# A sandwich layer (rotary linear attention, then a mixture of experts) on one core: transposes in pairs between products, the end in another order of products, its second weights split on the spot, and the residual of the early groups added by GpSimd

## The chip, the cores and the metric

One core of a Trainium2 chip. The kernel is one program with its own five instruction streams (TensorE is PE, its weight load PEld; VectorE is DVE; ScalarE is ACT; GpSimd is POOL; SyncE is SP and only issues transfers). The time is the device time of one execution in microseconds; lower is better.

## The reference, cut to what matters

X has 2 batches of 2048 tokens with 512 features, all in float32. `ln` is a layer norm over the features.

```
h   = ln(ln(X)) * ln_w + ln_b
Q, K, V = split(h @ W_in + b_in)           # 512 -> 3 * 512
Q, K = rope(Q), rope(K)
A   = sum over tokens of K / |K| * V       # one vector for a batch
x2  = X + ln(A * Q @ W_out + b_out + ln(X))
n3  = ln(x2)
gates: the two largest of n3 @ gate_w (8 experts), softmax over the two
routed = sum of gate * (gelu(n3 @ w1[e] + b1[e]) @ w2[e] + b2[e])
shared = gelu(n3 @ shared_w1 + shared_b1) @ shared_w2 + shared_b2
out = x2 + ln(routed + shared)
```

## The kernel before, in words

The 4096 tokens are 32 tiles of 128, in 8 groups of 4 tiles. Each float32 product is made of three products of split operands: a tensor is written as `hi` (rounded to float32r by an ACT copy) and `lo` (the rest, by a subtraction on DVE or POOL), and `product` (L1505) runs hi by hi, hi by lo and lo by hi over the 4 blocks of the contraction, so 12 matmuls of 512 columns. A "turn" brings a group from tokens on partitions to features on partitions by 16 transposes of 128 by 128, four to a PSUM bank, over two banks (`tp`). So the third set of four waits until the first bank has been emptied, and the fourth for the second.

**Front (0 to 322 us), a loop over 8 groups.** PE does for group g: for each of 4 tiles the K product and the V product (`kv`), then the turn of group g + 1, then four Q products (`q`, two banks). ACT empties the turn: for each k a copy with scale and bias into `hb`, and a rounding into `h_hi` (`front_split`), and POOL subtracts (`front_lo`, L1372), with two `hb` buffers, so the third ACT copy waits for POOL's first subtraction. ACT then takes the Q products out (`bias_q`) and rounds, in groups 1 to 5, four units of expert weights per group (`unit_hi`, L659: with tile 0, with tile 2, and behind Q products 0 and 2). DVE adds bias and rotates K, multiplies K by V, subtracts weight units (`unit_lo`, L943), and rotates Q together with POOL (`rc` on DVE at L925, `rsn` on POOL at L1391, which waits for Q products 0 and 1). Each engine takes its list in the order in which it is written. POOL adds K times V into `acc` (L1384).

**Attention (322 to 600 us), a loop over 8 steps.** Step s: four `attend` (a product with W_out and a bias row, into 3 banks), behind the third of them `n3_turn(s - 1)`, the transposes of the normed group before (`n3`, written by ACT at L714), then the gate's logits, and in most steps a quarter of the shared expert's work for the five EARLY groups (0, 2, 4, 6, 7): their first or their second product. ACT rounds the turn (`n_hi`), DVE subtracts (`n_lo_parts`, behind the third `z_tile`). Then the routing is worked out.

**Experts (627 to 893 us).** 71 tiles of 128 rows are gathered by indirect DMA, taken through their expert, and added into `f_scratch` by indirect DMA.

**The end (893 to 991 us).** The shared expert for the three LATE groups (1, 3, 5), as h0, o0, h1, o1, h2, o2 (`places`): `late_h(i)` is four products with the first shared weights, `late_turn(i + 1)` follows each h, `late_o(i)` is four products with the second weights (`c2_hi`, `c2_lo`, loaded ready split from scratch, 2 MB). Each h or o has four places m. Beside them DVE takes statistics of the EARLY tiles (`early_tile`, table `measured`; f is loaded by SP, one transfer of 1 MB for each group) and adds and measures the LATE ones (`late_tile`), POOL takes the roots (L1479), DVE the shifts, ACT norms the tile (`normed`, L827, table `normed_in`), and POOL issues a transfer that adds the tile to `out` in memory, where x2 lies already (`add_to_out`, L1486, 28 tiles). For the last group alone x2 is loaded (`x2c`), DVE adds it, and SP stores (L583). h and o of a group share one pair `hc_hi`, `hc_lo`, so ACT's first rounding of h(i) waits for the last product of o(i - 1).

Of the kernel before, what the change touches and what calls it, by code (L numbers as in the profile page):

```python
# [22 lines left out]
def sandwich_kernel(nc, X, ln_w, ln_b, W_in, b_in, W_out, b_out, gate_w, w1, b1, w2, b2,  # L23
# [51 lines left out]
    with ctx:  # L75
# [143 lines left out]
        hc_hi, hc_lo = at("hc_hi", 148, [P, KS, G], F32R), at("hc_lo", 156, [P, KS, G], F32R)  # L219
        x2c = at("x2c", 164, [P, GT, D])  # L220
# [51 lines left out]
        places = [(what, i, m) for i in range(len(LATE)) for what in ("h", "o") for m in range(GT)]  # L272
# [6 lines left out]
        measured = beside((0, 0, 2, 2, 1, 1, 1, 1, 2, 2, 2, 2, 1, 1, 1, 1) + (0,) * 8)  # L279
        normed_in = beside((0, 0, 0, 0, 0, 0, 2, 2, 0, 0, 1, 1, 2, 2, 2, 2, 1, 1, 1, 1, 1, 1, 0, 0))  # L280
# [20 lines left out]
        HALF_SET, ONES_SET, PICK_SET, GATE_ZERO, F_ZERO, ZEROS_SET = range(1, 7)  # L301
# [21 lines left out]
        bo_set, bo_hi_done, bo_split = sem("bo_set"), sem("bo_hi_done"), sem("bo_split")  # L323
        o_full, o_free, o_seen = sem("o_full"), sem("o_free"), sem("o_seen")
# [25 lines left out]
        c_in = [sem(f"c_in{i}") for i in range(3)]  # L350
# [5 lines left out]
        y_normed, y_added, stored, late_stored = sem("y_normed"), sem("y_added"), sem("stored"), sem("late_stored")  # L356
# [4 lines left out]
        def _(sp):  # L361
# [204 lines left out]
            sp.dma_start(c1_hi[:, :, :].rearrange("p k h -> p (k h)").bitcast(F32), ws_dram[0, 0]).then_inc(c_in[0], 16)  # L566

            for i in range(NRT - 1):
                sp.wait_ge(r_stored[i % NRO], 16 * (i // NRO + 1))
                sp.sem_inc(r_landed, 1)  # L570
            load_f(EARLY[0])
            load_f(EARLY[1])
            load_f(LATE[0])
            load_f(EARLY[2])
            load_f(EARLY[3])
            load_n3(2)
            load_f(LATE[1])
            load_f(EARLY[4])
            load_f(LATE[2])
            sp.dma_start(x2c[:, :, :], out_groups[LATE[2]]).then_inc(f_in[LATE[2]], 16)  # L580
            for j in range(GT):
                sp.wait_ge(y_added, j + 1)
                sp.dma_start(out_tiles[GT * LATE[2] + j], f[LATE[2]][:, j, :]).then_inc(late_stored, 16)  # L583
            sp.wait_ge(late_stored, 16 * GT)
            sp.wait_ge(stored, 16 * (NT - GT))

        @block.scalar
        def _(act):
# [9 lines left out]
            def front_split(f, u):  # L598
                for k in range(KD):
# [20 lines left out]
            def bias_q(g):  # L620
                for m in range(KD):
# [6 lines left out]
                    if m % 2 == 0:  # L628
                        unit_hi_in(g, 2 + m // 2)
# [41 lines left out]
            act.wait_ge(bo_set, 1)  # L671
# [141 lines left out]
            def gelu_c(i, m):  # L813
                n = KS * i + m
                act.wait_ge(sc_full, n + 1)
                if n >= 2:
                    act.wait_ge(hc_split, n - 1)
                act.activation(hsc[m % 2][:, :], sc[m if i == 0 else m % 2][:, :], ACT.Gelu, bias=sb1c[:, m:m + 1]).then_inc(sc_free, 1)
                if m == 0 and i > 0:
                    act.wait_ge(fc_full, GT * i)  # L820
                act.wait_ge(sc_free, n + 1)
                act.activation(hc_hi[:, m, :], hsc[m % 2][:, :], ACT.Copy).then_inc(hc_hi_done, 1)
# [7 lines left out]
            def load_c(n, i, c, w):  # L830
                act.dma_start(w[:, :, :].rearrange("p k h -> p (k h)").bitcast(F32), ws_dram[i, c]).then_inc(c_in[n], 16)
# [3 lines left out]
            load_c(1, 0, 1, c1_lo)  # L835
            scale_row(PRE)
            act.dma_start(n3c[1][:, :, :], n3_groups[LATE[1]]).then_inc(n3c_in[1], 16)
            load_c(2, 1, 0, c2_hi)
            load_c(2, 1, 1, c2_lo)
            for what, i, m in places:  # L840
                if what == "h":
                    gelu_c(i, m)
                if what == "h" and m == KS - 1 and i + 1 < len(LATE):
# [7 lines left out]
        def _(dve):  # L851
# [115 lines left out]
            for g in range(NG):  # L967
                k_tile(g, 0)
                v_tile(g, 0)
                if g == 0:  # L970
                    for n in range(2 * KD, 3 * KD):
                        lo_part(n)
                    dve.memset(bo[:, :].bitcast(F32), 0.0).then_inc(bo_set, 1)
                    dve.wait_ge(bo_hi_done, 1)
                    dve.wait_ge(bo_set, 1)
                    dve.tensor_tensor(bo[B_LO:B_LO + 1, :], bo_raw[B_LO:B_LO + 1, :], bo_hi[B_LO:B_LO + 1, :].bitcast(F32),
                                      ALU.subtract).then_inc(bo_split, 1)
# [78 lines left out]
            def n_lo_parts(g):  # L1056
                for k in range(KD):
# [38 lines left out]
            for s in range(NG):  # L1096
# [3 lines left out]
                z_tile(s, 1)  # L1100
                z_tile(s, 2)
                if s >= 1:
                    n_lo_parts(s - 1)
# [192 lines left out]
            def hc_lo_part(i, m):  # L1296
                dve.wait_ge(hc_hi_done, KS * i + m + 1)
                dve.tensor_tensor(hc_lo[:, m, :], hsc[m % 2][:, :], hc_hi[:, m, :].bitcast(F32), ALU.subtract)\
                   .then_inc(hc_split, 1)
# [16 lines left out]
            def early_tile(g, j):  # L1316
                if j == 0:
                    dve.wait_ge(f_in[g], 16)
# [15 lines left out]
            def add_x2(j):  # L1334
                g = LATE[-1]
                dve.wait_ge(y_normed, y_use[g, j] + 1)
                dve.tensor_tensor(f[g][:, j, :], f[g][:, j, :], x2c[:, j, :], ALU.add).then_inc(y_added, 1)

            waiting = []
            for what, i, m in places:  # L1340
                if what == "h":
                    hc_lo_part(i, m)
                else:
# [16 lines left out]
        def _(pool):  # L1360
# [120 lines left out]
            def add_to_out(g, j):  # L1481
                if g == LATE[-1]:
                    return
                pool.wait_ge(y_normed, y_use[g, j] + 1)
                pool.sem_inc(may_gather, 1)
# [13 lines left out]
        def _(pe):  # L1499
# [12 lines left out]
            def turn(f):  # L1512
                pe.wait_ge(h_normed, f + 1)
                for k in range(KD):
# [69 lines left out]
            def n3_turn(g):  # L1584
# [3 lines left out]
                for k in range(KD):  # L1588
# [47 lines left out]
            for s in range(NG):  # L1636
                attend(s, 0)
                attend(s, 1)
                attend(s, 2)
                if s >= 1:  # L1640
                    n3_turn(s - 1)
# [95 lines left out]
            for i in range(1, PRE + 1):  # L1737
# [5 lines left out]
                else:  # L1743
                    pe.wait_ge(n3c_in[0], 16)
# [29 lines left out]
            def late_h(i):  # L1774
                pe.wait_ge(tc_free, 4 + KD * (i + 1))
                if i == 0:
# [4 lines left out]
                    pe.wait_ge(c_in[1], 16)  # L1781
# [8 lines left out]
            def late_o(i):  # L1790
                pe.wait_ge(hc_split, KS * (i + 1))
                for j in range(GT):
# [3 lines left out]
                    product(oe_ps[n % 2][:, :], lambda k: hc_hi[:, k, c], lambda k: hc_lo[:, k, c],  # L1796
# [3 lines left out]
            pe.wait_ge(c_in[0], 16)  # L1800
            for i in range(len(LATE)):
                late_h(i)
                if i + 1 < len(LATE):
                    late_turn(i + 1)
                if i == 0:
                    pe.wait_ge(c_in[2], 32)
                late_o(i)
# [60 lines left out]
```

## Time and profile before

| | |
|---|---|
| median of 3 runs | 993.66 us (993.62 to 996.82) |
| the profiled execution's own time | 993.31 us |
| its span, first to last instruction | 991.5 us |
| PE busy | 894.3 us, 90% of the span |
| DVE, ACT, POOL busy | 632.4, 434.6, 399.7 us |
| mean granted TensorE clock | 0.974 of full speed |

The time holds about 2 us that lie outside the span. An idle gap of PE is read from PEld, the weight load that goes ahead of each matmul: the ends of matmuls are modelled and overlap the next start. In brackets behind a row stands how long its engine sat idle before it, and what ended that.

### The profile page before, as it was taken

Reading aid. Unit: us, or ns where it says so; the run is one execution under the profiler, and the core shown is the slowest. Engines: PE = TensorE matmul, PEld = TensorE weight load, DVE = VectorE, ACT = ScalarE, POOL = GpSimd, SP = SyncE. Lnnn points to the kernel's source line nnn. Section 1 sums busy time; section 2 is a strip of 40 time slices with the busy share of each in tenths; the row PEclk is TensorE's granted clock in tenths of the full one; section 3 lists DMA queues with packets and bytes.
Section 4 is the critical chain, followed back from the end, with each engine's and each line's share of the span. In section 5 each row is a group of like instructions: output and inputs, shape, how many; then the busy total and the mean of one; then the engine's idle time right before and its main releaser. Section 6 shows DMA issues by size and latency. Waiting matters only on the chain.

```text
span 991.5 us, 14758 instructions
## 1 busy us (share of the span) xinstructions
PE 894.3 (90%) x4558; PEld 733.2 (74%) x4558; DVE 632.4 (64%) x1358; ACT 434.6 (44%) x825; POOL 399.7 (40%) x328
## 2 busy tenths in 40 slices
PE   1998988988999899899999798699999999996985
PEld 1877877877878577677777686688888888884874
DVE  5757967966956755556566658466666566662774
ACT  4135345344342243131231435466666666663453
POOL 3356456455454000000000000376767676751463
PEclk9999999999999899999999999699999999999998
DMA  8226878778544795955533589387888777869988
GB/s 288 86 86 235 289 261 297 271 272 305 191 170 170 296 340 195 356 213 219 205 127 128 203 327 321 116 214 150 149 144 160 145 146 138 158 97 331 344 133 157
DMA packets 86842, 209.03 MB, mean 211 GB/s; under 512 B 11480, under 2 KB 19928, under 8 KB 81392
## 3 DMA queue, kind: packets, MB, share of 16 engines
q1 hardware_dynamic: 61760, 159.21, 44.4%
q0 software_dynamic: 19936, 44.65, 25.0%
q10 hardware_dynamic: 5072, 4.23, 1.5%
q8 instruction: 41, 0.67, 0.3%
q14 instruction: 33, 0.27, 0.1%
HBM read 117.05 MB, written 91.01 MB: 210 GB/s over the span
## 4 chain that ended last, share of the span: by engine, by line
PE 52%; DVE 9%; ACT 5%; DMA 5%; issue 3%; POOL 1%; DVEq 0%; ACTq 0%; SPq 0%; POOLq 0%
PE bank L1507 7%; PE bank L1508 7%; PE bank L1509 7%; PE bank L1703 4%; PE bank L1701 3%; PE bank L1702 3%; PE bank L1688 3%; PE bank L1718 3%; PE bank L1720 3%; PE bank L1719 3%; PE bank L1710 2%; DMA c_lo<-shared_scratch 2%; PE bank L1502 1%; DMA f_scratch<-fo 1%; PE bank L1621 1%
## 5 line engine op out<-in xcount | busy, mean ns | idle before, releaser
L1456 POOL DMA_INDIRECT f_scratch<-ro,dst x71 | 112.5, 1584 | 51.2 <-SPq L570 23.6
L1507 PE MATMUL bank<-wkv_hi,h_hi 128*128 128x512 f32 x256 | 100.6, 393 | 3.8 <-issue 3.8
L1448 POOL DMA_INDIRECT xr<-n_scratch,ids x71 | 70.0, 986 | 76.7 <-issue 48.4
L1508 PE MATMUL bank<-wkv_lo,h_hi 128*128 128x512 f32 x256 | 100.3, 392 | 0.0
L1509 PE MATMUL bank<-wkv_hi,h_lo 128*128 128x512 f32 x256 | 100.2, 391 | 0.0
L1260 DVE TENSOR_TENSOR ro<-bank,b2b 128x512 f32<-128x512 f32 x71 | 49.1, 692 | 65.7 <-PE bank L1720 54.3
L1701 PE MATMUL bank<-we,x_hi 128*128 x284 | 86.4, 304 | 0.3 <-DVE x_lo L1240 0.3
L1703 PE MATMUL bank<-we,x_lo 128*128 x284 | 80.5, 284 | 0.0
L1702 PE MATMUL bank<-we,x_hi 128*128 x284 | 80.5, 283 | 0.0
L613 ACT ACTIVATE sq<-kb 128x512 f32<-128x512 f32 x32 | 20.2, 633 | 117.1 <-DVE kb L905 117.1
L1377 POOL TENSOR_TENSOR rn<-ssq,half 128x1 f32<-128x1 f32 x32 | 27.5, 860 | 86.2 <-ACT sq L613 86.2
L1425 POOL TENSOR_TENSOR zr<-zv,half 128x4 f32<-128x4 f32 x8 | 8.1, 1009 | 134.1 <-DVE zv L1030 134.1
L1507 PE MATMUL bank<-wo_hi,q_hi 128*128 128x512 f32 x128 | 54.4, 425 | 7.4 <-DMA q_lo<-q_scratch 3.7
L1507 PEld LDWEIGHTS bank<-wkv_hi,h_hi 128*128 128x128 f32 x256 | 48.5, 190 | 14.3 <-issue 4.2
L1718 PE MATMUL bank<-we,g_hi 128*128 x142 | 56.5, 398 | 1.4 <-DVE g_lo L1252 1.3
L714 ACT ACTIVATE n<-z,xnm,xr__76 128x512 f32<-128x512 f32 x32 | 23.5, 804 | 77.2 <-DVE xnm L1053 77.2
L1507 PE MATMUL bank<-h_hi,wq_hi 128*128 128x512 f32 x128 | 51.3, 401 | 5.9 <-ACT qb L626 5.9
L1720 PE MATMUL bank<-we,g_lo 128*128 x142 | 56.4, 397 | 0.0
L1509 PEld LDWEIGHTS bank<-wkv_hi,h_lo 128*128 128x128 f32 x256 | 48.5, 189 | 10.2
L1719 PE MATMUL bank<-we,g_hi 128*128 x142 | 56.0, 394 | 0.0
L1508 PEld LDWEIGHTS bank<-wkv_lo,h_hi 128*128 128x128 f32 x256 | 48.5, 189 | 10.0
L1384 POOL TENSOR_TENSOR acc<-acc,prod 128x512 f32<-128x512 f32 x32 | 50.1, 1565 | 13.2 <-DVE prod L918 13.2
(226 smaller groups left out, 2523.0 us busy)
## 6 DMA issues: line engine op xcount, KB each, us to landing
xg<-in_X SPq DMA_DIRECT2D x16, 1024.0 KB, 7.8
we<-expert_scratch SPq DMA_DIRECT2D x6, 2048.0 KB, 12.6
w_lo<-in_w SPq DMA_DIRECT2D x16, 512.0 KB, 5.3
expert_scratch<-w_hi SPq DMA_DIRECT2D x16, 512.0 KB, 2.6
expert_scratch<-w_lo SPq DMA_DIRECT2D x16, 512.0 KB, 4.1
q_scratch<-qh SPq DMA_DIRECT2D x8, 1024.0 KB, 3.9
q_scratch<-qb SPq DMA_DIRECT2D x8, 1024.0 KB, 6.0
q_hi<-q_scratch SPq DMA_DIRECT2D x8, 1024.0 KB, 4.8
```

The costliest lines, as they stand in the source:

```text
L1384: pool.tensor_tensor(a, a, prod[j % 2][:, :], ALU.add).then_inc(acc_done, 1)
L1448: pool.indirect_dma_start(xr[u][:, :], None, n3_dram, bass.IndirectOffsetOnAxis(ids[:, i:i + 1], 0)).then_inc(row_in[u], 16)
L1456: pool.indirect_dma_start(f_dram, bass.IndirectOffsetOnAxis(dst[:, i:i + 1], 0), ro[i % NRO][:, :], None, compute_op=ALU.add).then_inc(r_s ...
L1507: pe.matmul(dst, hi(k), w_hi(k), start=(k == 0), stop=False)
L1508: pe.matmul(dst, hi(k), w_lo(k), start=False, stop=False)
L1509: last = pe.matmul(dst, lo(k), w_hi(k), start=False, stop=(k == KD - 1 and not more))
L1701: pe.matmul(out_h, x_hi[u][:, s], part_of(e, 0, k, H), start=(k == 0), stop=False)
L1702: pe.matmul(out_h, x_hi[u][:, s], part_of(e, 1, k, H), start=False, stop=False)
L1703: last = pe.matmul(out_h, x_lo[u][:, s], part_of(e, 0, k, H), start=False, stop=(k == KD - 1))
L1718: pe.matmul(oe_ps[u][:, :], g_hi[u][:, s], part_of(e, 2, k, D), start=(k == 0), stop=False)
L1719: pe.matmul(oe_ps[u][:, :], g_hi[u][:, s], part_of(e, 3, k, D), start=False, stop=False)
L1720: last = pe.matmul(oe_ps[u][:, :], g_lo[u][:, s], part_of(e, 2, k, D), start=False, stop=(k == KH - 1))
```

## The change: what it does

**Pairs of transposes.** In the front the first two sets of the turn of group g + 1 stand ahead of the last V product of group g and the other two behind Q product 0; in attention two sets stand ahead of the third `attend` and two ahead of the fourth. ACT takes the front's sets 0 and 1, Q product 0, sets 2 and 3, then Q products 1 to 3, with the weight units behind products 1 and 2; DVE takes `n_lo` in pairs ahead of and behind the third `z_tile`.

**The end.** The order is h0, h1, o0, h2, o1, o2, with two buffers of `hc_hi` and `hc_lo`; statistics and norms of EARLY tiles stand later in it (7 are measured by the end of o0, 11 in h2, 2 in o1; 10 of the 20 are normed in o1 and 4 in o2). `shared_w2` is loaded raw (1 MB) and split by ACT and DVE beside h1. For all five EARLY groups x2 is loaded by SP (5 MB more; statistics of a group now wait for f and x2), POOL adds it with 20 `tensor_tensor`, and SP stores those tiles; only the 8 tiles of groups 1 and 3 still go out by POOL's adding transfer. n3 of group 5 is loaded from ACT's queue, right behind the raw weights.

```diff
-        places = [(what, i, m) for i in range(len(LATE)) for what in ("h", "o") for m in range(GT)]
+        late_order = (("h", 0), ("h", 1), ("o", 0), ("h", 2), ("o", 1), ("o", 2))
+        places = [(what, i, m) for what, i in late_order for m in range(GT)]
-        measured = beside((0, 0, 2, 2, 1, 1, 1, 1, 2, 2, 2, 2, 1, 1, 1, 1) + (0,) * 8)
-        normed_in = beside((0, 0, 0, 0, 0, 0, 2, 2, 0, 0, 1, 1, 2, 2, 2, 2, 1, 1, 1, 1, 1, 1, 0, 0))
+        measured = beside((0,) * 6 + (2, 2, 0, 1, 1, 1, 2, 3, 3, 3, 1, 1) + (0,) * 6)
+        normed_in = beside((0,) * 8 + (0, 1, 1, 1, 1, 0, 1, 1, 2, 2, 3, 3, 2, 2, 0, 0))
...
             load_f(EARLY[0])
+            load_x2(EARLY[0])
+            load_f(LATE[0])
             load_f(EARLY[1])
-            load_f(LATE[0])
+            load_x2(EARLY[1])
...
+            sp.wait_ge(tc_full, 2 * KD)
+            load_x2(EARLY[3])
+            load_f(EARLY[4])
+            sp.wait_ge(tc_full, 3 * KD)
+            load_x2(EARLY[4])
             load_f(LATE[1])
-            load_f(EARLY[4])
+            sp.wait_ge(c_split, KS)
             load_f(LATE[2])
...
+            mine = [(g, j) for g, j in y_order if g not in LATE[:2]]
+            for g, j in mine[:6]:
+                store_y(g, j)
+            sp.wait_ge(sc_full, KS * len(LATE))
+            load_x2(LATE[2])
+            for g, j in mine[6:]:
+                store_y(g, j)
...
-                    front_split(g + 1, (g + 1) % 2)
-                    bias_q(g)
+                    front_split(g + 1, (g + 1) % 2, (0, 1))
+                    bias_q(g, (0,))
+                    front_split(g + 1, (g + 1) % 2, (2, 3))
+                    bias_q(g, (1, 2, 3))
...
                 pool.wait_ge(y_normed, y_use[g, j] + 1)
+                if g in EARLY:
+                    pool.tensor_tensor(f[g][:, j, :], f[g][:, j, :], x2c[g][:, j, :], ALU.add).then_inc(e_added, 1)
+                    return
                 pool.sem_inc(may_gather, 1)
                 pool.dma_start(out_tiles[GT * g + j], f[g][:, j, :], accum_op=ALU.add).then_inc(stored, 16)
...
+                    if j == GT - 1 and g + 1 < NG:
+                        turn(g + 1, (0, 1))
                     kv(g, j, 1)
-                if g + 1 < NG:
-                    turn(g + 1)
...
                 for m in range(KD):
                     q(g, m)
+                    if m == 0 and g + 1 < NG:
+                        turn(g + 1, (2, 3))
...
                 attend(s, 1)
+                if s >= 1:
+                    n3_turn(s - 1, (0, 1))
                 attend(s, 2)
                 if s >= 1:
-                    n3_turn(s - 1)
+                    n3_turn(s - 1, (2, 3))
```

## Rows read from the trace of the kernel before

**Rows 1.** Busy time by stretch: PE, PEld, DVE, ACT, POOL; clock; DMA share, GB/s.
```profile
400.00:500.00 100.00, 92.67 (x411) 71.22 (x410) 56.98 (x157) 26.56 (x41) 6.04 (x6) 0.98 0.63 235
...
910.00:920.00 10.00, 4.36 (x11) 3.48 (x12) 6.02 (x14) 0.09 (x1) 0.07 (x1) 0.66 1.05 388
...
940.00:950.00 10.00, 7.86 (x36) 6.42 (x35) 8.34 (x21) 5.36 (x9) 4.17 (x4) 0.83 0.70 126
```
**Rows 2.** Waits of the weight load, whole span: total, times, longest.
```profile
PEld bank L1502 <- ACT hb L604: 18.1, 16, 4.5
...
PEld bank L1502 <- DVE n_lo L1060: 13.8, 15, 2.3
...
PEld bank L1507 <- ACT qb L626: 8.8, 7, 1.6
```
**Rows 3.** Timeline of the weight load, front: turns and Q products.
```profile
51.76 0.42 PEld L1502 LDWEIGHTS bank<-ident,hn 128*128 128x128 f32 x4 [0.91 <-ACT hb L604]
58.24 0.19 PEld L1507 LDWEIGHTS bank<-h_hi,wq_hi 128*128 128x128 f32 x1 [0.76 <-ACT qb L626]
...
198.53 1.03 PEld L1502 LDWEIGHTS bank<-ident,hn 128*128 128x128 f32 x8
...
237.21 1.02 PEld L1502 LDWEIGHTS bank<-ident,hn 128*128 128x128 f32 x8
...
274.93 1.03 PEld L1502 LDWEIGHTS bank<-ident,hn 128*128 128x128 f32 x8
```
**Rows 4.** Timelines of POOL and DVE, groups 2 and 3 of the front.
```profile
131.82 2.61 POOL L1372 TENSOR_TENSOR h_lo<-hb,h_hi 128x512 fp32r<-128x512 f32 x2 [0.37 <-ACT h_hi L609]
...
134.63 1.23 DVE L943 TENSOR_TENSOR w_lo<-w_lo,w_hi 128x1024 fp32r<-128x1024 f32 x1 [7.04 <-ACT w_hi L659]
...
135.30 2.81 POOL L1391 TENSOR_TENSOR rsn<-qb,rf 128x1024 f32<-128x1024 f32 x1 [0.87 <-issue]
...
135.77 3.43 DVE L925 TENSOR_TENSOR rc<-qb,rf 128x1024 f32<-128x1024 f32 x1
...
147.71 0.69 DVE L896 TENSOR_TENSOR kb<-bank,bkv 128x512 f32<-128x512 f32 x1 [0.38 <-PE bank L1509]
```
**Rows 5.** Timeline of the weight load, attention, step 3.
```profile
415.87 0.18 PEld L1582 LDWEIGHTS bank<-bo,ones_f 64*128 64x128 f32 x1 [0.35 <-issue]
...
419.23 0.18 PEld L1582 LDWEIGHTS bank<-bo,ones_f 64*128 64x128 f32 x1 [0.35 <-issue]
...
421.88 0.42 PEld L1502 LDWEIGHTS bank<-ident,n 128*128 128x128 f32 x4 [1.37 <-DVE n_lo L1060]
```
**Rows 6.** Timeline of ACT, the same step.
```profile
414.16 2.94 ACT L714 ACTIVATE n<-z,xnm,xr__76 128x512 f32<-128x512 f32 x4 [21.05 <-DVE xnm L1053]
```
**Rows 7.** The end: timelines of ACT, DVE and the weight load.
```profile
908.05 2.04 ACT L790 ACTIVATE nc_hi<-bank 128x512 fp32r<-128x512 f32 x4
...
913.66 1.29 DVE L1319 BATCH_NORM_STATS2 fst<-f 128x6 f32<-128x512 f32 x2 [6.02 <-DMA f<-f_scratch]
914.86 0.68 DVE L1298 TENSOR_TENSOR hc_lo<-hsc,hc_hi 128x512 fp32r<-128x512 f32 x1
...
915.61 0.29 PEld L1507 LDWEIGHTS bank<-c_hi,hc_hi 128*128 128x128 f32 x1 [7.93 <-issue]
...
923.36 0.68 DVE L1329 TENSOR_TENSOR f<-bank,f 128x512 f32<-128x512 f32 x1
...
926.07 0.69 DVE L1329 TENSOR_TENSOR f<-bank,f 128x512 f32<-128x512 f32 x1
...
983.56 0.69 DVE L1329 TENSOR_TENSOR f<-bank,f 128x512 f32<-128x512 f32 x1
```
**Rows 8.** POOL's adds of 128 by 512 in the front: ns, least, median, most.
```profile
L1384 POOL TENSOR_TENSOR acc<-acc,prod x32: 1262/1292/2210, 42.7 to 314.2; 128x512 f32<-128x512 f32 x32
```
**Rows 9.** Timeline of POOL in the end.
```profile
933.18 5.34 POOL L1486 DMA_DIRECT2D out<-f  x6
...
985.47 0.57 POOL L1479 TENSOR_TENSOR fr<-fv,half 128x1 f32<-128x1 f32 x1 [1.31 <-DVE fv L1307]
```

More of the change, by code:

```diff
@@ L218, in sandwich_kernel @@
         hsc = [at(f"hsc{i}", 144 + 2 * i, [P, G]) for i in range(2)]
-        hc_hi, hc_lo = at("hc_hi", 148, [P, KS, G], F32R), at("hc_lo", 156, [P, KS, G], F32R)
-        x2c = at("x2c", 164, [P, GT, D])
+        hc_hi, hc_lo = ([at(f"{n}{i}", kb_ + 24 * i, [P, KS, G], F32R) for i in range(2)] for n, kb_ in (("hc_hi", 148), ("hc_lo", 156)))
+        x2c = {g: at(f"x2c{g}", kb_, [P, GT, D]) for g, kb_ in zip(EARLY + LATE[-1:], (164, 96, 128, 64, 72, 136))}
+        c2_raw = at("c2_raw", 8 * LATE[-1], [P, KS, D])
         fst, fmv = at("fst", 192.125, [P, NT, 6]), at("fmv", 193, [P, NT, 2])
@@ L348, in sandwich_kernel @@
         gate_ready, r_gated, r_landed = sem("gate_ready"), sem("r_gated"), sem("r_landed")
-        c_in = [sem(f"c_in{i}") for i in range(3)]
+        c_in, c_hi_done, c_split = [sem(f"c_in{i}") for i in range(2)], sem("c_hi_done"), sem("c_split")
         n3c_in, f_in = [sem(f"n3c_in{i}") for i in range(len(LATE))], [sem(f"f_in{g}") for g in range(NG)]
@@ L570, in _, with load_x2, store_y @@
                 sp.sem_inc(r_landed, 1)
+            def load_x2(g):
+                sp.dma_start(x2c[g][:, :, :], out_groups[g]).then_inc(f_in[g], 16)
+            def store_y(g, j):
+                if g in EARLY:
+                    sp.wait_ge(e_added, e_tiles.index((g, j)) + 1)
+                else:
+                    sp.wait_ge(y_added, j + 1)
+                sp.dma_start(out_tiles[GT * g + j], f[g][:, j, :]).then_inc(y_stored, 16)
             load_f(EARLY[0])
+            load_x2(EARLY[0])
+            load_f(LATE[0])
             load_f(EARLY[1])
-            load_f(LATE[0])
+            load_x2(EARLY[1])
             load_f(EARLY[2])
+            load_x2(EARLY[2])
             load_f(EARLY[3])
-            load_n3(2)
+            sp.wait_ge(tc_full, 2 * KD)
[3 more added lines that the diff above has]
+            load_x2(EARLY[4])
             load_f(LATE[1])
-            load_f(EARLY[4])
+            sp.wait_ge(c_split, KS)
             load_f(LATE[2])
[L580 to L585, printed above, removed]
+            mine = [(g, j) for g, j in y_order if g not in LATE[:2]]
[5 more added lines that the diff above has]
+                store_y(g, j)
+            sp.wait_ge(y_stored, 16 * len(mine))
+            sp.wait_ge(stored, 16 * 2 * GT)
         @block.scalar
@@ L596, in hi_part, with front_split @@
                 act.activation(dst, stage[n][:, :], ACT.Copy).then_inc(w_hi_done, 1)
-            def front_split(f, u):
-                for k in range(KD):
+            def front_split(f, u, ks=range(KD)):
+                for k in ks:
                     n = KD * f + k
@@ L618, in unit_hi_in, with bias_q @@
                     unit_hi(UG * (g - 1) + i)
-            def bias_q(g):
-                for m in range(KD):
+            def bias_q(g, ms=range(KD)):
+                for m in ms:
                     n = q_use(g, m)
@@ L818, in gelu_c @@
                 act.activation(hsc[m % 2][:, :], sc[m if i == 0 else m % 2][:, :], ACT.Gelu, bias=sb1c[:, m:m + 1]).then_inc(sc_free, 1)
-                if m == 0 and i > 0:
-                    act.wait_ge(fc_full, GT * i)
+                if m == 0 and i > 1:
+                    act.wait_ge(fc_full, GT * (i - 1))
                 act.wait_ge(sc_free, n + 1)
-                act.activation(hc_hi[:, m, :], hsc[m % 2][:, :], ACT.Copy).then_inc(hc_hi_done, 1)
+                act.activation(hc_hi[i % 2][:, m, :], hsc[m % 2][:, :], ACT.Copy).then_inc(hc_hi_done, 1)
             def normed(g, j):
@@ L842, in _ @@
                     gelu_c(i, m)
+                if (what, i) == ("h", 1):
+                    c2_hi_part(m)
                 if what == "h" and m == KS - 1 and i + 1 < len(LATE):
@@ L1054, in x2_shift, with n_lo_parts @@
                    .then_inc(xnm_ready, 1)
-            def n_lo_parts(g):
-                for k in range(KD):
+            def n_lo_parts(g, ks=range(KD)):
+                for k in ks:
                     n = t2_use(g, k)
@@ L1336, in add_x2, with c2_lo_part @@
                 dve.wait_ge(y_normed, y_use[g, j] + 1)
-                dve.tensor_tensor(f[g][:, j, :], f[g][:, j, :], x2c[:, j, :], ALU.add).then_inc(y_added, 1)
+                dve.tensor_tensor(f[g][:, j, :], f[g][:, j, :], x2c[g][:, j, :], ALU.add).then_inc(y_added, 1)
+            def c2_lo_part(k):
+                dve.wait_ge(c_hi_done, k + 1)
+                dve.tensor_tensor(c2_lo[:, k, :], c2_raw[:, k, :], c2_hi[:, k, :].bitcast(F32), ALU.subtract)\
+                   .then_inc(c_split, 1)
             waiting = []
@@ L1510, in product, with turn @@
                 return last
-            def turn(f):
+            def turn(f, ks=range(KD)):
                 pe.wait_ge(h_normed, f + 1)
-                for k in range(KD):
+                for k in ks:
                     n = KD * f + k
@@ L1587, in n3_turn @@
                     pe.wait_ge(tp_free, 2 + KD * NG)
-                for k in range(KD):
+                for k in ks:
                     n = t2_use(g, k)
@@ L1795, in late_o @@
                     c = slice(j * P, (j + 1) * P)
-                    product(oe_ps[n % 2][:, :], lambda k: hc_hi[:, k, c], lambda k: hc_lo[:, k, c],
+                    product(oe_ps[n % 2][:, :], lambda k: hc_hi[i % 2][:, k, c], lambda k: hc_lo[i % 2][:, k, c],
                             lambda k: c2_hi[:, k, :], lambda k: c2_lo[:, k, :]).then_inc(fc_full, 1)
             pe.wait_ge(hc_free, NRT - 1)
[L1800 to L1807, printed above, removed]
+            for what, i in late_order:
+                if what == "h":
+                    late_h(i)
+                    if i + 1 < len(LATE):
+                        late_turn(i + 1)
+                else:
+                    if i == 0:
+                        pe.wait_ge(c_split, KS)
+                    late_o(i)
 _NAMES = ["X", "ln_w", "ln_b", "W_in", "b_in", "W_out", "b_out"]
```

48 lines of the change are left out of this document (27 added, 21 removed).

## The prediction, on record before the changed kernel ran

> **What bounds the kernel now.** First I read the page's busy time: PE is the fullest engine, so I looked for its gaps. The busy time by stretch shows PE 92.7% busy in attention and, in the end, ten us with 4.4 busy [rows 1]. The list of waits says what the weight load waited for [rows 2]: in the front 18.1 us for ACT's `hb` (the third and fourth set of each turn) and 8.8 us for ACT's `qb` (the third Q product), in attention 13.8 us for DVE's `n_lo`. The timelines then tell which of these gaps are worth their length. A gap of PE is worth it only if PE, once early, finds nothing else late, so I asked of each stretch how long the next engine idles.
>
> In the front PE repeats in 37.7 us (237.21 to 274.93; 38.7 where the sum over `acc` is added) [rows 3]. In the same 37.7 us DVE idles 7.04 us for one weight unit and 0.38 us for PE, and hardly otherwise [rows 4]. The 7.04 us are no slack. They are the way from DVE's last K times V through POOL's adds and subtractions (two wait for one another through the two `hb` buffers) to ACT's two sets of the turn, one Q product taken out, and the weight unit, for which DVE waits ahead of `rc`. That ring, DVE, POOL, ACT, DVE, is a second bound 0.38 us under PE's.
>
> **Front, groups 1 to 5.** The pairs end the turn's gaps, and product 2 of Q no longer waits: product 3 does, for `bias_q(1)`, which now stands where `bias_q(0)` stood. PE runs one product (2.7 us, 12 matmuls; the spacing of the end's products shows it [rows 7]) ahead. But the ring stays: weight unit 2 still comes behind one Q copy behind all four sets. What can move in it is `rsn`. Before, POOL was done with `h_lo` at 134.43 and waited 0.87 us for `bias_q(1)`; now it starts at 134.5, just ahead of DVE's `w_lo` at 134.63 [rows 4]. Would that shorten the ring? `rc` took 3.43 us because `rsn` ran: it ended 1.1 us behind it [rows 4]. If `w_lo` is held off in the same manner, it ends at 138.4 and `rc` at 139.6, against 139.2 before: the 0.38 us won is lost. If DVE is first, `rc` ends at 139.05 and the ring wins 0.5 us. I take 0.25 us for each of the four rounds, 1.0 us, between 0 and 0.85 + 0.38 = 1.2 us a round if nothing were held off (4.9 us).
>
> The Trainium skill (GPSIMD Engine Reference, Specifications) says that GpSimd's SBUF interfaces are shared with VectorE and that instructions of VectorE with two SBUF inputs contend; `w_lo` and `rc` have two. By that rule the round wins nothing (973 to 974 us); without it the sum would be 3.9 us lower (970 us).
>
> **Front, its two ends.** Turn 1 has no weight units beside it and DVE there waits for PE, so its gaps count: 0.91 and 0.76 us [rows 3] and one like the 0.91, less what remains at product 3: 2.3 us. The 0.96 us of the sum over `acc` (38.7 less 37.7) falls into PE's new lead: 1.0 us. Behind group 5 no unit is left, PE bounds again and cashes its lead of one product, 2.7 us, and 0.6 us of the last turn's gaps. Front: 2.3 + 1.0 + 1.0 + 3.3 = 7.6 us, not the 20 us that the list of waits offers. Bounds: 5, if a round loses as much as it may, and 12.
>
> **Attention.** Each of seven turns loses 1.37 to 1.58 us and a gap of 0.18 to `n_lo` [rows 2, 5]. DVE is busy 57 us of 100 here, PE 92.7 [rows 1], so PE is the bound and the gaps count. With an `attend` (3.36 us from bias row to bias row [rows 5]) between the pairs, the four odd steps win 1.55 us; in the three even ones DVE starts its `z` late behind ACT's last `hs_hi`, and 0.3 of 1.76 us stay. The new wait is for `n3`, wanted one `attend` earlier. In step 3 ACT ends it at 417.10 [rows 6] and the turn began at 419.65, now 416.3: 0.8 to 0.9 us lost. The other steps have it in time (the closest by 0.1 us). So 4 x 1.55 + 3 x 1.46 - 0.9 = 9.7, I take 9.5 us, between 6 (a wait for `n3` in each odd step) and 11. Everything behind, the last transfer of weights included, is released by PE's progress and moves along; the 71 expert tiles keep their time.
>
> **The end, PE's side** (clock times as in the trace before). The largest gap, 7.93 us, ended not with the weights but with DVE's fourth `hc_lo` (914.86), which stood behind a tile statistic that waited 6.02 us for f [rows 7]. The new order takes that away. It bares another: h1 now comes right behind turn 1, and needs all four `nc_lo`. ACT's `nc_hi` ran from 908.05 for 2.04 us [rows 7], DVE is 0.6 behind: h1 starts at 910.8, a gap of 3 us. Around a gap of PE at 943.9 the granted clock was 0.83 over ten us [rows 1], 1.7 us lost; I charge that again. So h1 ends at 923.4, turn 2 at 925.1, o0 waits for the raw weights' last `c2_lo` to 926.0, and four blocks of 10.9 us bring h2 to an end at 947.9, o1 at 958.8 and o2 at 969.7. Before, o2 ended just ahead of DVE's last add of f at 983.56 [rows 7]: 13.6 us. The raw load is 1 MB where two were, and ready. The 5 MB more of x2 share the DMA engines, which move a load of 1 MB in 2.7 us (388 GB/s [rows 1]): group 7's pair is the fifteenth from about 900 on and lands at 941, at 944 with the first adding transfers between, and is wanted at 951.
>
> **The end, DVE and POOL.** In h2 DVE has 11 statistics at 0.65 (1.29 for two [rows 7]), four `hc_lo` at 0.6, two group variances at 0.57 and shifts, 11.7 us in 10.9; a place of o with one statistic takes 2.7 us [rows 7]. Followed place by place, the last early variance (group 7) is written at 959.2 instead of 956.5. From there POOL, in order, has 14 of its 20 adds (2, 2, 3, 3, 2, 2 from o1 on), four adding transfers and seven roots, and the four roots on which the last tiles wait stand between them. An add of this size took 1.29 us in the median [rows 8], a transfer 0.89 (5.34 for six), a root 0.57 [rows 9]: 14 x 1.29 + 4 x 0.89 + 7 x 0.57 = 25.6 us, so the last root is done at 984.8. Before, it was done at 986.0 and the span ended 5.5 us later; 1.1 us of that tail was DVE behind its add of the tile before, which now comes early: 4.4 us. The end is 989.2, a gain of 2.3 us of the 13.6 that PE wins. POOL becomes the bound. Bounds: adds at 2.21 us, the longest row [rows 8], cost 12.9 us more; were POOL in time, the gain is 12 to 13.6.
>
> The Trainium skill (GPSIMD Engine Reference, Engine selection) speaks against this part: an elementwise add with two inputs is about twice as slow on GpSimd as on VectorE. Twice DVE's 0.69 us add [rows 7] is 1.38 us, an estimate by that page; the row says 1.29. By the page the sum would be 1.3 us higher.
>
> **The sum.** 7.6 + 9.5 + 2.3 = 19.4 us off the profiled execution's 993.3 us gives 973.9; the median of the runs is 0.35 us above the profiled one, so 974 us.
>
> **The rivals.** (1) POOL keeps up, because DVE measures group 7 at PE's pace or adds and issues overlap: the end wins 12, 964 us. For it: POOL idles until 956 and could start sooner. Against it: the order, which puts ten adds into o1's norms. 0.17. (2) The front's ring gives way (`w_lo` is not held off, or unit 2 comes sooner): 4 to 5 us more, 969 us. For it: where `rsn` and `rc` start together DVE lost nothing. Against it: `rc`'s 3.43 us. 0.13. (3) The adds meet DVE's work with two SBUF inputs or the queue is late with x2: 1.7 us an add instead of 1.29, 5.7 us more, 980 us, up to 987 at 2.21. Against it: in o1 and o2 DVE has few instructions with two inputs in SBUF. 0.16. (4) Slower than before: the same POOL row, long enough to eat all. 14 adds would have to cost 1.4 us more each, 2.7 us, to bring 993 back, and 3.1 us for 998. The longest add of 32 took 2.21. 0.03. (5) The turns bring nothing at all, since DVE takes their place in attention too: 991 us. 0.03. DVE's 57 busy us of 100 in attention speak against it.
>
> **How the numbers follow.** The forecast has 0.48: 970 to 978 us. The range takes in (2) and nearly all of (1) and (3): 964 to 984 us. A measurement of this kernel tells about 0.5% from no change, 5 us. Faster by more than that: all but (4), (5) and the worst of (3): 0.94; within: 0.03; slower: 0.03.
>
> **What would show it.** Front: the turn's second pair without a gap in PEld, a wait of 1 to 2 us ahead of Q product 3, DVE's wait for the weight unit still near 7 us, the round near 37.5 us in groups 1 to 5. Attention: the `n_lo` waits near 2 us in sum but for the last turn, a wait for `n3` in step 3. End: a 3 us gap ahead of h1 for `nc_lo` and a lower clock behind it, none of 7.9 us; POOL's adds near 1.3 us, POOL without idle time over the last 25 us, DVE's shifts and ACT waiting for roots. Wrong if the rounds of the front fall to 36 us, or if the last roots follow their variances at once.

## The result, and the profile after

The changed kernel takes 985.61 us (median of 4 runs, 984.49 to 986.89) against 993.64 us (4 runs) for the kernel before: ratio 0.991, interval 0.989 to 0.994. It is faster by 0.9%, 8 us, where 974 us and at worst 984 us were forecast. Its profiled execution took 984.49 us with a span of 982.7 us.

One row divides the kernel. ACT issues the load of `c_lo` when PE is done with the last expert tile; both kernels have it, and only the end lies behind it. First the row of before, then that of after (timeline of ACT's queue):

```profile
892.66 0.34 ACTq L831 DMA_DIRECT2D c_lo<-shared_scratch  x1
```
```profile
873.42 0.34 ACTq L862 DMA_DIRECT2D c_lo<-shared_scratch  x1
```

Up to here 19.2 us are won (17.1 were forecast). From here to the end of the span it is 982.7 - 873.4 = 109.3 us, against 991.5 - 892.7 = 98.8 before: the end, forecast to win 2.3 us, **lost 10.4**. Everything that is missing is missing there. The stretches of the end, after (the columns are those of [rows 1]):

```profile
930.00:940.00 10.00, 6.18 (x28) 4.78 (x26) 8.79 (x19) 4.14 (x6) 3.62 (x4) 0.99 0.47 106
940.00:950.00 10.00, 7.53 (x24) 6.07 (x25) 9.42 (x32) 2.23 (x3) 6.87 (x7) 0.67 0.43 142
950.00:960.00 10.00, 5.62 (x25) 4.32 (x23) 9.76 (x9) 2.93 (x4) 10.00 (x11) 1.00 0.76 197
960.00:970.00 10.00, 8.51 (x24) 6.51 (x24) 9.72 (x13) 5.05 (x7) 7.96 (x10) 0.66 0.61 165
```

PE, said to run through o1 and o2, is busy 5.6 to 8.5 of ten us in the last three rows. DVE looks like the bound with 9.8 of ten in 950 to 960, but with nine instructions: the ten us before have 32. So its timeline comes next (start, duration, instruction), and POOL's beside it:

```profile
928.35 2.27 DVE L1329 TENSOR_TENSOR hc_lo<-hsc,hc_hi 128x512 fp32r<-128x512 f32 x1 [1.01 <-ACT hc_hi L848]
...
935.15 1.88 DVE L1345 TENSOR_TENSOR fnm<-fnm,znm 128x4 f32<-128x4 f32 x1
...
947.54 0.17 DVE L1338 TENSOR_SCALAR fv<-fmv 128x4 f32<-128x4 f32 x1
...
953.31 7.06 DVE L1344 SCALAR_TENSOR_TENSOR fnm<-fmv,fr 128x1 f32<-128x1 f32 x1
...
964.23 7.25 DVE L1344 SCALAR_TENSOR_TENSOR fnm<-fmv,fr 128x1 f32<-128x1 f32 x1
```
```profile
952.39 2.85 POOL L1524 TENSOR_TENSOR f<-f,x2c 128x512 f32<-128x512 f32 x2
954.89 0.85 POOL L1517 TENSOR_TENSOR fr<-fv,half 128x1 f32<-128x1 f32 x1
955.42 1.20 POOL L1527 DMA_DIRECT2D out<-f  x1
956.06 4.28 POOL L1524 TENSOR_TENSOR f<-f,x2c 128x512 f32<-128x512 f32 x3
962.38 0.57 POOL L1517 TENSOR_TENSOR fr<-fv,half 128x1 f32<-128x1 f32 x1 [2.04 <-DVE fv L1338]
...
968.39 3.07 POOL L1524 TENSOR_TENSOR f<-f,x2c 128x512 f32<-128x512 f32 x2
...
976.60 0.55 POOL L1517 TENSOR_TENSOR fr<-fv,half 128x1 f32<-128x1 f32 x1
```

A shift of one element per partition, 0.15 us where POOL adds nothing, took 7.06 us. It ended at 960.37; POOL's row of adds, begun before it (with a root and the issue of a transfer in its middle), ended at 960.34. The next took 7.25 us and ended at 971.48, POOL's adds at 971.46. Both inputs of such a shift lie in SBUF, and so do those of the `hc_lo` (2.27 us, else 0.69) and the 128x4 shift (1.88, else 0.16). The variances (L1338, one SBUF tensor) and the adds of PSUM and SBUF were not held. Behind DVE waited PE, and ACT behind the shifts (waits of the whole kernel, of after):

```profile
ACT f L853 <- DVE fnm L1345: 41.7, 11, 11.4
...
PEld bank L1548 <- DVE f L1360: 12.7, 2, 6.7
```

This suggests a culprit at once, and the experiments show how much of it is cause and how much is shadow. In what follows "after the issue" counts from that `c_lo` row of the run's own trace.

### The profile page after: what moved, and what is told of

Its sections match the earlier page's. It is cut to its first block, busy times and chain, and to the rows that moved or that the text cites. A ratio compares the mean times of both kernels' runs of the same rounds, so it can differ in the third digit from the quotient of the medians.

```text
span 982.7 us, 14783 instructions
## 1 busy us (share of the span) xinstructions
PE 892.8 (91%) x4558; PEld 734.5 (75%) x4558; DVE 652.7 (66%) x1362; ACT 435.8 (44%) x829; POOL 405.4 (41%) x328
## 4 chain that ended last, share of the span: by engine, by line
PE 47%; DVE 13%; issue 6%; ACT 5%; POOL 3%; DMA 3%; DVEq 0%; POOLq 0%; ACTq 0%
PE bank L1548 5%; PE bank L1549 4%; PE bank L1550 4%; PE bank L1748 4%; PE bank L1746 3%; PE bank L1747 3%; PE bank L1733 3%; PE bank L1763 3%; PE bank L1765 3%; PE bank L1764 3%; PE bank L1755 2%; DVE fnm L1344 2%; PE bank L1543 2%; ACT n L740 1%; DMA f_scratch<-fo 1%
## 5 line engine op out<-in xcount | busy, mean ns | idle before, releaser
L972 DVE TENSOR_TENSOR w_lo<-w_lo,w_hi 128x1024 fp32r<-128x1024 f32 x20 | 34.5, 1725 | 35.2 <-ACT w_hi L683 35.2
```

## The experiments

Each ratio is to the kernel before on the same chip. Its median was 994.2 us beside the first four runs (`turns_only`, `end_only`, `no_pool_add`, `shifts_one_input`), 995.3 beside `psum_norm`, `dve_adds`, `three_groups` and `unit2_early`, and 990.6 beside the rest, so between these groups the ratios are compared and not the times.

**Which part loses: `turns_only` and `end_only`.** The diff cut in two. `turns_only` has the `ks=(0, 1)`, `ks=(2, 3)` turns of front and attention and ACT's `bias_q` to match, and the old end; `end_only` all the rest.

> The kernel before with the pairs of transposes alone (front and attention); the end is the old one. The theory (the whole of the difference to my forecast lies in the new end): the 19.2 us that the kernel after shows up to the load of the second weights arrive at the end undiminished, 993.6 - 19.2 = 974.4 us, ratio 0.980. The rival (what turns win, the tail of the kernel gives back, whatever its order): about 985 us, ratio 0.991.

> The kernel before with the new end alone; front and attention as before. The theory: the new end costs 10.4 us (109.3 us from the last load on ACT's queue to the end of the span, 98.8 before), so 1004 us, ratio 1.010. The rival, my forecast's step on the end (it wins 2.3 us, and the loss in the kernel after comes from the turns moving it): 991 us, ratio 0.998.

Measured: turns alone 976.1 us, ratio 0.981 (0.979 to 0.983); the end alone 1004.2 us, ratio 1.009 (1.007 to 1.011). Both within 2 us of the theory. The parts add up (0.981 x 1.009 = 0.990), so the turns give 18 of their 19.2 us at the end too, and the new end costs 9 to 10 by itself. The kernel with half of the change is 9.5 us faster than with all of it.

**No adds on POOL: `no_pool_add`.** The early tiles go out by POOL's adding transfer, as before the change, and their x2 is not loaded.

```
-                if g in EARLY:
-                    pool.tensor_tensor(f[g][:, j, :], f[g][:, j, :], x2c[g][:, j, :], ALU.add)...
-                    return
                 pool.dma_start(out_tiles[GT * g + j], f[g][:, j, :], accum_op=ALU.add)...
```

> The kernel after, but POOL adds nothing: the five early groups' tiles go out by POOL's adding transfer as before, and their x is not loaded. The new order of products, the new tables of statistics and norms and the split second weights stay. The theory (POOL's adds hold off DVE's small instructions and delay the roots): about 966 us, 962 to 970, ratio to before 0.972; DVE's shifts back at 0.2 us or less. The rival (the order and its tables cost it, whatever POOL does): 982 us or more, ratio 0.988 or above.

Measured 981.7 us, ratio 0.987 (0.985 to 0.989): the theory's 966 is missed, and the time lies next to the rival's bound. The trace tells why this is not the rival's reason. The shifts are back at 0.15 us, PE is done 21 us before the span ends, and then (stretches of this run):

```profile
950.00:960.00 10.00, 6.75 (x30) 5.26 (x28) 5.60 (x19) 6.74 (x10) 10.00 (x17) 1.00 1.12 190
960.00:970.00 10.00, 0.00 (x0) 0.00 (x0) 4.02 (x11) 1.64 (x3) 4.37 (x6) 0.51 1.11 228
970.00:978.00 8.00, 0.00 (x0) 0.00 (x0) 0.00 (x0) 0.00 (x0) 0.00 (x0) 0.50 0.60 137
```

the DMA engines are full with adding transfers (28 tiles instead of 8) at 190 to 228 GB/s. The span ends 12 us past DVE's last add (966.3). The transfers fill the first 8 of these, to about 974; what the rest waits for is not shown. I had taken one bound away and put another in its place.

**The long shifts: `shifts_one_input` and `psum_norm`.** In the first the shifts read one tensor, the other operands as scalars per partition. In the second, besides, ACT norms the last group into PSUM, so that DVE's last adds have only one SBUF tensor.

```
-                done(dve.scalar_tensor_tensor(fnm[...], fmv[..., 0], -1.0, fr[...], ALU.mult, ALU.mult))
-                dve.tensor_tensor(fnm[...], fnm[...], znm[...], ALU.add)
+                for c in range(n):   # fng = -mean, one more instruction beside fv
+                    dve.tensor_scalar(fnm[c], fng[c], fr[c], znm[c], ALU.mult, ALU.add)
...
-                act.activation(f[g][:, j, :], f[g][:, j, :], ...)
+                dst = tc[j][:, :] if g == LATE[-1] else f[g][:, j, :]
+                act.activation(dst, f[g][:, j, :], ...)
```

> The kernel after, with POOL's adds kept, but DVE computes the shifts of the early tiles with instructions that read one SBUF tensor and take the others as per-partition scalars (one instruction a tile and one for the negated means, where two instructions had two tensors each). The theory (the two waits of 7 us in front of DVE's shifts are the loss): 974 to 978 us, ratio to before 0.980 to 0.984. The rival (POOL's own length, roots in order behind adds, is the bound and DVE's long shifts are its shadow): 983 to 986 us, ratio 0.989 to 0.992.

> The kernel with one-input shifts (984.3 us), and besides ACT writes the norms of the last group's four tiles to PSUM, so that DVE's last adds of x read PSUM and one SBUF tensor in place of two SBUF tensors. In the run with one-input shifts alone the 7 us that DVE had lost at a shift were lost at the first of these adds (6.56 us in place of 0.69). The theory (any DVE instruction with two SBUF tensor inputs is held off for as long as POOL's adds stand back to back): that add is back at 0.7 us, DVE has no such instruction left after h2, and the end comes 5 to 7 us sooner, 978 us (976 to 980), ratio 0.983. The rival (POOL's row of adds and roots in order is the bound, DVE's long instructions only its shadow): 983 to 985 us, ratio 0.990.

Measured 984.3 us (0.989, 0.987 to 0.991), the rival's number, and 983.2 us (0.987, 0.984 to 0.989): the rival's time, but on a chip on which the kernel before took 995.3 us, so that the ratio lies halfway between the theory's 0.983 and the rival's 0.990. DVE's timeline in the first:

```profile
963.53 0.27 DVE L1347 TENSOR_SCALAR fnm<-fng,fr,znm 128x1 f32<-128x1 f32 x1 [2.99 <-POOL fr L1520]
...
968.62 0.28 DVE L1347 TENSOR_SCALAR fnm<-fng,fr,znm 128x1 f32<-128x1 f32 x1 [2.89 <-POOL fr L1520]
968.80 6.64 DVE L1371 TENSOR_TENSOR f<-f,x2c 128x512 f32<-128x512 f32 x1
```

and in the second:

```profile
966.62 0.27 DVE L1348 TENSOR_SCALAR fnm<-fng,fr,znm 128x1 f32<-128x1 f32 x1 [3.00 <-POOL fr L1521]
...
971.71 0.28 DVE L1348 TENSOR_SCALAR fnm<-fng,fr,znm 128x1 f32<-128x1 f32 x1 [2.89 <-POOL fr L1521]
971.90 0.68 DVE L1372 TENSOR_TENSOR f<-bank,x2c 128x512 f32<-128x512 f32 x1
```

The mechanism is real: the one-input shift slips past POOL, the hold of 7 us goes to the next instruction with two SBUF tensors, and with that one gone too nothing is held in o1 and o2. But little is won, since the freed DVE waits 3 us at a time for POOL's next root, which stands behind the same adds. In `psum_norm` POOL runs without a gap from group 7's variance (953.20) to its last root (978.49): 25.3 us. The forecast's row, made of the same 14 adds, had 25.6, and in the kernel after the row took 29.6. So of the 14 us that DVE was held in o1 and o2 about 4 reached the end; the rest was the shadow of POOL's own length. Nor did the profiled `psum_norm` keep these 4 us whole, it lost 2.7 ahead of the row: its variance of group 7 came 953.2 - 876.4 = 76.8 us after the issue, against 74.1. Its o0 alone began 35.9 us after the issue, against 34.5.

**Adds elsewhere: `dve_adds`, `three_groups`, `adds_left_out`.** `dve_adds` moves the twenty adds to DVE, one place behind the norm; `three_groups` leaves 12 to POOL and gives the tiles of groups 6 and 7 to adding transfers; in `adds_left_out` POOL only signals, so that twenty tiles of the output lack x; the loads of x2 and the stores stay, so they are not what this run wins by.

```
                 if g in EARLY:
-                    pool.tensor_tensor(f[g][:, j, :], f[g][:, j, :], x2c[g][:, j, :], ALU.add).then_inc(e_added, 1)
+                    pool.sem_inc(e_added, 1)
                     return
```

> The kernel after, but DVE adds x to the twenty early tiles (0.6 us each, 12 us in all, one place behind the norm) and POOL only computes roots and issues eight adding transfers. Order, tables, loads and buffers as in the kernel after. The theory (POOL's adds are the loss, by their length and by holding DVE off): DVE was idle about 15 us of the last 60 in the run without the adds and takes them nearly within these gaps; 971 us (968 to 975), ratio 0.977. The rival (order and tables are the loss): 982 us or more, since the adds now also lengthen DVE.

> The kernel after, but POOL adds only the tiles of the first three early groups (12 adds); the tiles of groups 6 and 7 (8) go out by POOL's adding transfer and their x is not loaded. The run without any adds ended with 11.7 us in which only the adding transfers of 28 tiles still ran (DMA engines full from 948 us on), the kernel after with POOL 8 us late. The theory (both ends of the scale are bounds, POOL's adds at one and the DMA engines at the other): between them it is faster than both, 974 us (970 to 978), ratio 0.980. The rival (the order and its tables are the loss): 981 to 985 us.

> The kernel after, but POOL's twenty adds are left out: the early tiles are stored as ACT normed them, without x, so the twenty tiles of the output lack that term. Order, tables, loads, stores, roots and the eight adding transfers as in the kernel after. So far: adds on DVE 977.4 us, on POOL 985.6. The theory (adds cost the end by their length in POOL's order and by what they hold off): 969 us (966 to 973), ratio 0.974, and the variance of group 7 about 4 us earlier after the c_lo load's issue than the 74.1 us of the kernel after. The rival (most of the loss is the order with its tables): 978 us or more.

Measured: 977.4 us, 0.981 (0.979 to 0.983), for DVE's adds, 6 us off the estimate (4 by the ratios) but far from the rival: they took 0.68 us each and stood in front of PE's tiles (PE waited up to 4.0 us for DVE's `f`). Without adds 965.0 us, 0.974 (0.971 to 0.977), the theory's ratio (in us it lies under the theory's 966 to 973, on a chip with a faster kernel before). Against the kernel after (0.991) that is 17 us: what POOL's adds cost in all. `three_groups` refutes its theory: 986.2 us, 0.990 (0.987 to 0.993), no gain over the kernel after. One hold of 5.83 us stayed in o1, PE waited 10.8 us for DVE in all, and the eight further adding transfers then came in a bunch; DVE's last add ended at 975.1 and the span at 983.8.

**When the statistics come: `early_tables`, `mix_old_tables`, `mix`.** Another table of statistics and norms, with nothing else changed in `early_tables`. In `mix`, besides, the tiles of groups 0, 2 and 4 go out by adding transfer, those of 6 and 7 are added by DVE; `mix_old_tables` is `mix` with the tables of the kernel after.

```
-        measured = beside((0,) * 6 + (2, 2, 0, 1, 1, 1, 2, 3, 3, 3, 1, 1) + (0,) * 6)
-        normed_in = beside((0,) * 8 + (0, 1, 1, 1, 1, 0, 1, 1, 2, 2, 3, 3, 2, 2, 0, 0))
+        measured = beside((0,) * 6 + (2, 2, 0, 1, 1, 4, 3, 3, 3, 1) + (0,) * 8)
+        normed_in = beside((0,) * 8 + (0, 1, 1, 1, 1, 1, 2, 2, 2, 2, 2, 2, 1, 1, 1, 0))
```

> The kernel after with other tables: DVE measures 10 of the early tiles before h2 in place of 7 and the other 10 in h2 in place of 11, two statistics no longer stand in o1; ACT norms 9 early tiles before o1 in place of 7. POOL's adds as in the kernel after. In the run without POOL's adds DVE idled 4.2 us in h2 behind ACT's copies of gelu and POOL's root with the statistics queued behind. The theory (the row of POOL that ends the kernel begins 7.6 us later than my forecast had it, because the last statistics are late; its own 25 to 29 us are as forecast): the variance of group 7 comes 5 us sooner, two adds leave the row, 979 us (976 to 982), ratio 0.984. The rival (POOL's hold on DVE decides, wherever the statistics stand): 984 us or more.

> As the mixed kernel (groups 0, 2 and 4 by adding transfer, 6 and 7 added by DVE), with the tables of the kernel after. The theory (late statistics cost the end several us, whoever adds): 4 to 6 us slower than with the other tables, 972 us (969 to 976), ratio 0.978. The rival (tables make no difference, the tail is set by the transfers): within 1 us of the mixed kernel.

> The kernel after with the other tables and no add on POOL: the tiles of groups 0, 2 and 4 go out by POOL's adding transfer (no load of x), those of groups 6 and 7 are added by DVE (8 adds of 0.6 us). It spreads the work over what the runs so far showed to be the bounds: POOL's row (985.6), the adding transfers of 28 tiles at 200 to 270 GB/s (981.7), twenty adds of DVE (977.4). The theory (each of them was the bound in its run, and PE is done with o2 at about 953 if none is): 967 us (963 to 972), ratio 0.973, faster than the kernel with the turns alone and the old end (976.1). The rival (the new order itself costs what it was to win): 976 us or more.

Measured: 979.1 us, 0.988 (0.987 to 0.990): the time expected, but on a chip on which the kernel before took 990.6, so that by the ratios 3 us are won where 6 were expected; 970.9 us, 0.980 (0.978 to 0.982); and 964.7 us, 0.972 (0.970 to 0.974). The tables (which norm 9 tiles ahead of o1 in place of 6, not of 7 as written above) are worth 3 us while POOL adds, and 6 (medians) to 8 us (ratios) once it doesn't. In `early_tables` the variance came 4.8 us sooner, but POOL's row behind it took 970.7 - 939.5 = 31.2 us in place of 29.6, with holds of DVE of 3.2, 2.8 and 4.8 us in it. `mix` is the fastest of the kernels that give the whole output, 26 us under the kernel before on its chip and 9 us by the ratios under the turns alone. So the new end does win 9 us, when POOL has none of the adds and the tables are the other ones.

**The front's ring: `unit2_early`.**

```
-                    if m in (1, 2):
-                        unit_hi_in(g, 1 + m)
+                    if m in (0, 2):
+                        unit_hi_in(g, 2 + m // 2)
```

> The kernel after, but ACT computes weight unit 2 behind the first Q copy and unit 3 behind the third (before the change it was so), where the kernel after has them behind the second and the third. My account of the front (the ring DVE, POOL, ACT, DVE over unit 2 is the bound in groups 2 to 5, with DVE waiting 7 us for it): the rounds of 37 us fall to 35 to 36 us, 4 to 8 us off, 979 us, ratio 0.985. The rival (the rounds are bound by DVE's held-off work itself, and the unit is only where the wait shows): the unit's Copy ahead of the third set delays PE by up to 0.7 us a round, 985 to 988 us.

Measured 987.7 us, 0.992 (0.990 to 0.995): nothing won. The gaps at the second pair are gone, but the rounds of groups 2 to 5 took 38.5, 36.1, 39.6 and 36.0 us, 37.5 in the mean, against 37.1 in the kernel after. DVE no longer waits 7 us for the unit, but (DVE's timeline, then POOL's):

```profile
126.06 1.42 DVE L972 TENSOR_TENSOR w_lo<-w_lo,w_hi 128x1024 fp32r<-128x1024 f32 x1 [1.04 <-ACT w_hi L683]
132.18 1.76 DVE L954 TENSOR_TENSOR rc<-qb,rf 128x1024 f32<-128x1024 f32 x1 [4.69 <-ACT qb L650]
136.26 0.69 DVE L956 TENSOR_TENSOR qb<-rc,rsn 128x512 f32<-128x512 f32 x1 [2.33 <-POOL rsn L1429]
```
```profile
132.81 3.35 POOL L1429 TENSOR_TENSOR rsn<-qb,rf 128x1024 f32<-128x1024 f32 x1
```

it waits the same 7 us for the Q copy and for `rsn`.

## Why the prediction was wrong, step by step

**The end, DVE and POOL: the step that failed.** The end as a whole was to win 2.3 us and lost 10.4. The forecast's row of POOL's work, in order, had the right length (25.6 us; 29.6 measured, 4.1 of them idle, so 25.5 of work). What failed is the time at which that row begins, and the term, put at nothing, for what POOL's adds do to DVE. In us after the issue: the variance of group 7 was to be written at 959.2 - 892.7 = 66.5 and came at 947.5 - 873.4 = 74.1, 7.6 late; from there to the end of the last root 25.6 were forecast and 29.6 taken; the tail was 5.5 in place of 4.4, since DVE still stood at earlier adds: the last shift began 1.2 us behind its root, as it had before (1.1). (The 956.5 beside the forecast's 959.2 is no row of before, where that variance was written at 959.8; the sum does not use it.) 7.6 + 4.0 + 1.1 = 12.7 us, the whole distance between 2.3 us won and 10.4 lost.

The 7.6 us have two parts, told apart by `adds_left_out`, where the variance came at 942.2 - 871.5 = 70.7. So 3.4 us are holds of DVE by POOL's adds in h2: the `hc_lo` of 2.27 us and the shift of 1.88, 1.6 + 1.7 us above their ordinary lengths. The other 4.2 us remain without any add. They are idle time that "11.7 us in 10.9" did not contain: that term summed DVE's work and left out that `hc_lo` stands first in each place, so that the statistics behind it wait for ACT's copy of the gelu (2.28 and 1.01 us) and for POOL's root (0.94), 4.2 us together. The kernel before shows such waits in its own last h (DVE's timeline):

```profile
962.32 0.69 DVE L1298 TENSOR_TENSOR hc_lo<-hsc,hc_hi 128x512 fp32r<-128x512 f32 x1 [2.37 <-ACT hc_hi L822]
```

There no statistic stood behind them; the new tables put eleven there. Moving statistics in front of h2 brought the variance to 69.3 in `early_tables` and from 69.8 to 62.5 between the two mixed kernels.

The row's 4.0 us are the two holds of 7 us. While DVE stood, no variance was written, and POOL, its adds done, idled 2.04 us twice ahead of a root; without holds (`psum_norm`) the row was 25.3. Rival (3) named the meeting of adds and two-input work and gave it 0.16, but priced it as longer adds, 1.7 us each. The 14 adds took 19.4 us, 1.38 each; it was DVE that paid. That 985.6 us lies in that rival's stretch (980 to 987) is luck, since the adds did not cost what it charged. What I set against it, that DVE has few instructions with two SBUF inputs in o1 and o2, was the mistake. Few and tiny they are, but one can stand for a whole row of adds, and the step had counted adds by their own length only. The Trainium skill (GPSIMD Engine Reference, Specifications) says that instructions of VectorE with two SBUF inputs contend with GpSimd; the trace agrees (0.15 us became 7.06 and 7.25), and I had weighed that page for the front alone. That the adds cost 17 us is still mainly their length: `psum_norm`, without a hold in o1 and o2 (one `hc_lo` of 2.46 us in h2 stayed), gave back 2 us by the medians and 5 by the ratios.

**The end, PE's side.** The 7.93 us gap went, and the gap ahead of h1 came near the forecast (3.7 for 3 us, with a granted clock of 0.83 in 890 to 900), as did the wait ahead of o0 for the split second weights:

```profile
892.64 0.29 PEld L1816 LDWEIGHTS bank<-nc_hi,c_hi 128*128 128x128 f32 x1 [3.73 <-DVE nc_lo L1295]
907.91 0.19 PEld L1548 LDWEIGHTS bank<-c_hi,hc_hi 128*128 128x128 f32 x1 [1.26 <-DVE c_lo L1372]
```

o0 began 34.5 us after the issue; forecast 33.3. Of the 13.6 us on PE's side `mix` collects more than half: its end takes 965.2 - 874.0 = 91.2 us after the issue, 7.6 less than before. The loads of x2 were in time, as said; `turns_only` still shows the old gap of 7.91 us.

**Attention.** 9.5 us forecast, 9.2 measured (19.2 to the issue less the front's 10.1). The wait list no longer has `n_lo` but for the last turn, as forecast:

```profile
PEld bank L1543 <- ACT n L740: 3.0, 3, 2.0
PEld bank L1543 <- DVE n_lo L1089: 2.1, 1, 2.1
```

Nor is the wait for `n3` as new as that row makes it look: 1.97 of the 3.0 us stand at the last turn, in both kernels. New are 0.74 us in step 1, where the forecast had none, and 0.25 in step 3, where it had 0.9.

**Front.** 7.6 us forecast, 10.1 measured: the wait for `q_lo` ahead of attention ended at 330.3 against 340.3. The rounds between turns took 34.4, 35.0, 37.1, 37.1, 38.0 and 36.2 us; before they took 36.7, 37.7, 37.7, 37.7, 38.7 and 37.7. Nearly all of the 2.5 us above the forecast lies in the second, one of the four that were to win 0.25 us each: it won 2.7. The last came close to the 36 us that were to show the account wrong. DVE waited 7.0 us for the weight unit, as said, and `w_lo` was held off by `rsn` as forecast: its 20 instructions averaged 1725 ns, 1220 before. `rc` gave that back, its 8 instructions averaged 1351 ns in place of 2600. In turns 3 to 5 gaps stay at the second pair, which were to be closed, 0.5 us ahead of it and 0.9 between its two sets:

```profile
115.00 1.02 PEld L1543 LDWEIGHTS bank<-ident,hn 128*128 128x128 f32 x8
...
121.83 0.42 PEld L1543 LDWEIGHTS bank<-ident,hn 128*128 128x128 f32 x4 [0.54 <-issue]
123.16 0.42 PEld L1543 LDWEIGHTS bank<-ident,hn 128*128 128x128 f32 x4 [0.91 <-ACT hb L628]
...
152.11 1.02 PEld L1543 LDWEIGHTS bank<-ident,hn 128*128 128x128 f32 x8
```

The second bound exists, but not where I put it: `unit2_early` takes the weight unit out and the rounds do not shrink in the mean. DVE waits for the way over POOL (`acc`, `h_lo`, `rsn`) and ACT's Q copies; the unit was only the place where that wait showed. Which of these sets the round was not tried.

## What to carry to other kernels

Work given to POOL costs three times: its own length in POOL's order, the small results (here the roots) queued behind it, and the VectorE instructions with two SBUF tensors that fall into it, however small (here 3.4 us in h2 and 4.1 in o1 and o2 reached the end). Sum the work of a block place by place with its waits, not as busy time: an instruction that waits at the head of each place makes the work behind it late although there is room on paper. And when one bound is lifted, price the next before calling the edit useless: with the tables of the kernel after, twenty tiles on POOL gave 0.991, on adding transfers 0.987, on DVE 0.981, and the split between transfers and DVE 0.980, which is not clear of DVE alone. With the other tables the split gave 0.972 and POOL 0.988; DVE alone was not tried with them.

## What the hardware showed that I had not expected

In the kernel after, a small VectorE instruction with two SBUF tensors that met GpSimd's adds of 128x512 ended 0.02 to 0.03 us behind the end of one of them, in `three_groups` too (960.48 against 960.45). How many adds it stood for varied. Twice it was the whole row, 7.06 and 7.25 us, with a GpSimd root and the issue of a transfer among the adds. But 4 us earlier a shift got in between two adds that follow each other at once (one ended at 950.06), and the next shift stood for the second (POOL's row, then DVE's two):

```profile
948.77 2.52 POOL L1524 TENSOR_TENSOR f<-f,x2c 128x512 f32<-128x512 f32 x2
949.36 0.72 DVE L1344 SCALAR_TENSOR_TENSOR fnm<-fmv,fr 128x1 f32<-128x1 f32 x1
950.11 1.21 DVE L1345 TENSOR_TENSOR fnm<-fnm,znm 128x1 f32<-128x1 f32 x1
```

What decides between the two is not shown. The same arithmetic with one tensor and scalars per partition took 0.27 us in the place of the long holds. GpSimd suffered little from them: its row, less its idle time, took 25.5 us with the two holds and 25.3 without (`psum_norm`).
